# Linear attention and a routed feed-forward on one core: two blocks of transpositions moved to the head of their steps

## What is computed

```python
x = x + linear_attention(layernorm(x, g1, b1), Wq, Wk, Wv, Wo)   # 16 heads of 64, phi = elu + 1,
h = layernorm(x, g2, b2)                                          # causal sums over keys and values
x = x + gelu(h @ Wf1) @ Wf2
x = layernorm(x_in + x)
x = layernorm(x + mixture(x))     # 8 experts of width 512, the best 2 for each token
```

## Time and profile before

| | |
|---|---|
| median of 3 runs | 686.7 us (686.63 to 686.72) |
| the profiled execution's own time | 687.75 us |
| its span, first to last instruction | 686.0 us |
| TensorE busy | 651.0 us, 95% |
| VectorE busy | 530.8 us, 77% |
| ScalarE busy | 426.8 us, 62% |
| GpSimd busy | 247.1 us, 36% |
| mean granted clock of TensorE | 0.998 |

### The profile page before, as it was taken

One profiled execution on the slowest core, in us unless ns is written; L12 is line 12 of the kernel. 1 busy time (PEld: TensorE's weight loads), 2 busy tenths in 40 slices (PEclk: granted clock), 3 DMA queues, 4 the chain that ended last, 5 costly groups with the idle time before them and its releaser, 6 DMA issues.

```text
span 686.0 us, 23205 instructions
## 1 busy us (share of the span) xinstructions
PE 651.0 (95%) x9330; PEld 558.5 (81%) x9330; DVE 530.8 (77%) x1565; ACT 426.8 (62%) x862; POOL 247.1 (36%) x274
## 2 busy tenths in 40 slices
PE   3899999999999999999999999999988999999995
PEld 2678888888888788888888887877878989999983
DVE  4877788887888788888878886888788677665674
ACT  4565676558556856765585568566646666666646
POOL 6300014025313512340253134123306657766664
PEclk9999999999999999999999999999999999999999
DMA  7340010001100100100011000001031233354536
GB/s 246 106 77 18 2 33 17 18 19 49 32 10 25 49 19 18 48 18 17 19 49 33 10 27 15 18 18 33 2 96 48 72 95 118 106 156 127 171 129 185
DMA packets 46521, 40.27 MB, mean 59 GB/s; under 512 B 9104, under 2 KB 41232, under 8 KB 46416
## 3 DMA queue, kind: packets, MB, share of 16 engines
q1 hardware_dynamic: 35360, 25.25, 13.2%
q0 software_dynamic: 4784, 10.39, 4.4%
q10 hardware_dynamic: 6272, 3.16, 1.6%
HBM read 23.12 MB, written 15.66 MB: 57 GB/s over the span
## 4 chain that ended last, share of the span: by engine, by line
PE 67%; DVE 18%; ACT 8%; issue 2%; POOL 2%; DMA 1%; DVEq 0%; ACTq 0%; POOLq 0%
PE banks_o L736 9%; PE banks_sc L571 5%; PE banks_o L551 4%; PE banks_o L563 3%; PE bank_u L584 3%; PE bank_u L544 3%; DVE work L1275 3%; PE bank_q L438 3%; DVE work L1291 3%; PE bank_q L440 3%; PE bank_q L439 3%; PE bank_k L438 2%; ACT work L916 2%; PE banks_sc L438 2%; PE banks_sc L450 2%
## 5 line engine op out<-in xcount | busy, mean ns | idle before, releaser
L1743 POOL DMA_INDIRECT routed_rows<-routed,slot x64 | 63.2, 988 | 144.9 <-PE banks_sc L571 113.4
L842 ACT ACTIVATE work<-bank_u 128x384 f32<-128x384 f32 x64 | 31.5, 492 | 98.8 <-PE bank_u L584 98.5
L1291 DVE TENSOR_TENSOR work<-banks_sc,causal 128x1024 f32<-128x1024 f32 x64 | 77.7, 1214 | 0.0
L736 PE MATMUL banks_o<-w,work 128*128 x624 | 76.2, 275 | 0.0
L736 PEld LDWEIGHTS banks_o<-w,work 128*128 128x128 f32 x624 | 73.0, 192 | 0.3 <-issue 0.2
L551 PE MATMUL banks_o<-v_aug,work 128*64 128x65 f32 x2048 | 70.6, 221 | 0.0
L1711 POOL TENSOR_SCALAR ve<-mv 128x4 f32<-128x4 f32 x24 | 4.7, 196 | 170.1 <-DVE mv L1157 169.9
L551 PEld LDWEIGHTS banks_o<-v_aug,work 128*64 128x64 f32 x2048 | 65.3, 138 | 0.0
L1275 DVE SCALAR_TENSOR_TENSOR work<-bank_q,work 128x512 f32<-128x512 f32 x64 | 43.7, 683 | 22.8 <-ACT work L910 22.7
L1275 DVE SCALAR_TENSOR_TENSOR work<-bank_k,work 128x512 f32<-128x512 f32 x64 | 44.2, 690 | 21.7 <-ACT work L916 21.6
L571 PE MATMUL banks_sc<-work 64*64 64x128 f32 (+1 forms) x2048 | 56.8, 248 | 1.2 <-ACT v_aug L842 0.7
(11 more groups left out here) (331 smaller groups left out, 1807.7 us busy)
## 6 DMA issues: line engine op xcount, KB each, us to landing
work<-in_L_attn_x SPq DMA_DIRECT2D x16, 256.0 KB, 3.7
work<-routed_rows SPq DMA_DIRECT2D x20, 132.0 KB, 2.4
xg_more<-routed_rows SPq DMA_DIRECT2D x19, 132.0 KB, 2.1
stage<-in_L_ffn_w SPq DMA_DIRECT2D x8, 256.0 KB, 2.5
moe_input<-routed SPq DMA_DIRECT2D x8, 256.0 KB, 2.6
work<-moe_input ACTq DMA_DIRECT2D x8, 256.0 KB
v_aug<-expert_results SPq DMA_DIRECT2D x4, 512.0 KB, 6.4
out<-work SPq DMA_DIRECT2D x6, 256.0 KB, 2.9
```

What stands on the lines that cost most here:

```text
L736: mm = pe.matmul(Y[t % 2][:, blk(k)], hTe[t % 2][:, f, blk(k)], w2[:, bass.ds(e[t] * F + f * D, D)], start=(f == 0), stop=(f == NF - 1))
L1291: dve.tensor_tensor(am_all.rearrange("p (x m) s -> p x (m s)", m=2), sc_banks.rearrange("p (x s) -> p x s", s=2 * P), causal[:, :, :].rear ...
L1743: pool.indirect_dma_start(rows_d, bass.IndirectOffsetOnAxis(slot[:, k, c:c + 1], 0), routed[:, c, k, :], None).then_inc(sct, 16)
```

## The change

In step 2 the four transpositions of `y_t(b-1)` and their wait stand ahead of `columns(g-1)`, not behind it. In step 3 those of `front_t(b+1)` do so too, and they go to bank_q, not bank_k; their wait for the bank is `a_free` in place of `b_free`. `front_scale` reads bank_q. The wait for `h32_sb` stands ahead of `q_proj`, not `k_proj`. The call for the first sequence, ahead of all steps, keeps bank_k. Nothing is computed differently.

```diff
-            def front_t(b):
+            def front_t(b, out):
                 pe.wait_ge(ln_x[0], b + 1)
...
-                        mm = pe.transpose(bkB[:, blk(c)], xln[:, c, :], ident)
+                        mm = pe.transpose(out[:, blk(c)], xln[:, c, :], ident)
...
+                if p == 2 and not first:
+                    a_free(g - 1)
+                    y_t(b - 1, bkA)
+                if p == 3 and not last:
+                    a_free(g - 1)
+                    front_t(b + 1, bkA)
                 if g > 0:
                     columns(g - 1)
-                    if p == 2 and not first:
-                        a_free(g - 1)
-                        y_t(b - 1, bkA)
-                    if p == 3 and not last:
-                        b_free(g - 1)
-                        front_t(b + 1)
                     across(g - 1)
...
+                    if p == 3 and not last:
+                        pe.wait_ge(h32_sb, b + 2)
                     if g == 0:
                         pe.wait_ge(wlo, 5)
                     q_proj(npar, np_)
...
                 if nxt:
-                    if p == 3 and not last:
-                        pe.wait_ge(h32_sb, b + 2)
...
                     k_proj(npar, np_)
...
-                act.activation(h32, bkB[:, :], ACT.Identity, bias=cols[:, 1:2], scale=cols[:, 0:1]).then_inc(h32_sb, 1)
+                act.activation(h32, src[:, :], ACT.Identity, bias=cols[:, 1:2], scale=cols[:, 0:1]).then_inc(h32_sb, 1)
...
-                    front_scale(b + 1, True)
+                    front_scale(b + 1, True, bkA)
```

More of the change, by code:

```diff
@@ L470, in front_t @@
                     if c % 2 == 0:
-                        mm = pe.transpose(bkB[:, blk(c)], xln[:, c, :], ident)
+                        mm = pe.transpose(out[:, blk(c)], xln[:, c, :], ident)
                     else:
-                        mm = pe.matmul(bkB[:, blk(c)], xln[:, c, :], exchange, start=True, stop=True)
+                        mm = pe.matmul(out[:, blk(c)], xln[:, c, :], exchange, start=True, stop=True)
                 mm.then_inc(f1_mm, 1)
@@ L686, in _ @@
             pe.wait_ge(cst, 3)
-            front_t(0)
+            front_t(0, bkB)
             pe.wait_ge(cst, CST_ALL)
@@ L849, in y_copy, with front_scale @@
                 copy(to[:, :, 1, DH:P], at[:, :, 1, 0:DH]).then_inc(yT_sb, 1)
-            def front_scale(b, reuse):
+            def front_scale(b, reuse, src):
                 act.wait_ge(f1_mm, b + 1)
@@ L993, in _ @@
             act.wait_ge(ld_cols, 16 * 2)
-            front_scale(0, False)
+            front_scale(0, False, bkB)
             front_high(0, 0)
```

## The result

The changed kernel takes 690.96 us (median of 4, 690.56 to 692.25), the kernel before 686.71 beside it. The ratio on record is 1.0051, 95% interval 1.0034 to 1.0069: 3.5 us slower, between 2.3 and 4.7. The forecast was 691.2. The profiled execution took 690.85 us, with a span of 689.1.

The account below looks back on a forecast made before the run. The prediction took a chain through VectorE, ScalarE and GpSimd to bound steps 2 and 3, despite TensorE 95% busy. Six sequences at 0.20 + 0.52 us plus 0.20 made 4.5 us, so 691.2, range 688.6 to 693.2.

Parts of the forecast that it names:

- The chain: Steps 2 and 3 of a sequence: VectorE, ScalarE and GpSimd set the end, with TensorE on the chain only for h2_t's 0.67 us.
- the signs named: Expected in the profile: TensorE and VectorE waits in steps 2 and 3, norm2 no longer behind GpSimd, sequences 63.6 us apart.
- Step 2: y_t ahead of the columns: columns 0.90 us later, a cover of 0.70, so the states 0.20 us late per sequence.
- Step 3: front_t ahead of the columns: columns 0.94 us later, norm2's wait takes 0.42, and 0.52 us per sequence is left.
- The sum: Sequences 1 to 6 at 0.72 us each, sequence 7 at 0.20: together 4.5 us slower.
- Edits counted at nothing: The moved h32_sb wait, b_free to a_free and SyncE's load cost nothing; the first sequence 0, within 0.3 us.
- The faster one: Whole change: fewer passages between large and small matmuls on a stream TensorE bounds, 2.9 us faster, 683.8; chance 4%.
- Rival 2: The same or nearly: the states' lateness falls into waits in steps 2 and 3; 1.2 us slower, 687.9; chance 8%.
- Rival 3: Step 3: norm2's wait takes nothing because GpSimd is as late as VectorE; 7.0 us slower, 693.7; chance 8%.

Follow-up runs that it names:

- y_twice_new: The changed kernel with y_t's four transpositions issued twice, ahead of the columns: 694.66 us, ratio to before 1.0118, spacing 63.95 us.
- y_twice_old: The kernel before with y_t's four transpositions issued twice, in the old place behind the columns: 687.75 us, ratio 1.0014, spacing 62.90 us.
- y_only: The kernel before with only y_t moved ahead of the columns, measured twice: 689.51 and 689.59 us, ratios 1.0035 and 1.0032.
- bank_only: The changed kernel with both blocks back behind the columns, keeping the bank and wait edits: 686.86 us, ratio to before 0.9998.
- twice_first_new: The changed kernel with GpSimd's sum (L1721) ahead of the factor from the statistics in step 2: 690.41 us, ratio to before 1.0053.
- ffn_order: The kernel before with ffn1's second and third products exchanging banks in step 3, so the one waiting for k_phi comes third: 687.31 us, ratio 0.9997.
- order_and_twice: The kernel before with both the edit of ffn_order and that of twice_first: 684.74 us, ratio to before 0.9954.
- front_only: The changed kernel with y_t back behind the columns, so only front_t is moved, with its bank_q: 691.08 us, ratio to before 1.0044.
- twice_first: The kernel before with GpSimd's sum (L1721) ahead of the factor from the statistics in step 2: 686.82 us, ratio 0.9994.

## Why the prediction was right

**The chain.** Right. Steps 2 and 3 were bound by VectorE, ScalarE and GpSimd, and TensorE's work moved ahead of L544 went onto it (`y_twice_new` against `y_twice_old`). Of the signs named, these came: TensorE's waits ahead of `y_t` (0.24) and of the first weight load of `front_t` (0.23), VectorE's idle time ahead of the states in step 3 (0.80, forecast 0.9), `norm2` without idle time, a spacing of 63.5. The row of the states in step 2 shows no idle time, where 0.2 was forecast: `k_phis` ended at 150.16 and they started at 150.28, 0.12 later.

**Step 2.** Right in each stamp. With the shift of 0.53, `y_t` was forecast at 149.08 and came at 149.07; the columns at 149.66 and came at 149.66; the states at 150.28 and came at 150.28. Cost 0.20; `y_only` shows 0.21.

**Step 3.** Right down to `norm2`. With the shift of 0.73: `front_t` forecast 156.28, measured 156.28; columns 157.15, measured 157.10; states 157.77, measured 157.71; `norm2` 159.02, measured 158.98.

**The term that was mis-sized** is the last of that step: I took `norm2`'s lateness, 0.52, as that of `h2_t`. `h2_t` started at 160.14, where 159.05 + 0.73 + 0.52 would be 160.30. It is 0.36 late. Of the 0.16 too much, 0.04 come from the start of `norm2` and 0.11 from its length: 1.22 us in the earlier trace rows and 1.11 in the changed kernel. I had counted that length as fixed.

It is not the wait that makes `norm2` long, though the two go together in the earlier trace rows. In the kernel before, `norm2` of sequence 1 waits too and takes 1.11, and the same four instructions in `front_apply` take 1.24 without a wait:

```profile
94.93 1.11 DVE L1163 TENSOR_SCALAR work<-work,mv,rstd 128x128 f32<-128x128 f32 x4 [0.28 <-POOL work L1721]
...
145.93 1.24 DVE L1163 TENSOR_SCALAR work<-work,mv,rstd 128x128 f32<-128x128 f32 x4
146.18 0.96 POOL L1743 DMA_INDIRECT routed_rows<-routed,slot  x1 [0.30 <-issue]
...
157.91 1.07 POOL L1743 DMA_INDIRECT routed_rows<-routed,slot  x1 [0.17 <-issue]
```

What goes with the length is GpSimd: in all thirteen profiles, from 20 us on, wherever such a group of four takes 1.21 to 1.24, one of GpSimd's scatter instructions (L1743) starts 0.13 to 0.25 us behind its start, and in no group of 1.10 to 1.12 does one start in its first 0.6 us. In the changed kernel the scatter's instruction starts at 158.64, 0.34 ahead of `norm2`. That the one causes the other was not tested. Sequence 1, which has no scatter beside `norm2`, fits: there `scale2` comes 0.51 later behind `residual1` than before, and the forecast's term was 0.52.

So a sequence costs 0.20 + 0.36 = 0.56 and not 0.72. The middle distances give 63.48 - 62.90 = 0.58.

**The sum.** Worked out anew, the steps come to 6 x 0.56 + 0.20 = 3.6 us, against 4.5 forecast. In the profiles they hold 3.9: from the first `residual1` to the last `scale2` 390.08 us (88.05 to 478.13) against 386.45, so 3.63, and ahead of that 0.2 in step 2 of sequence 1 and 0.08 in sequence 0. The 0.3 above the terms lies at the edges, which I took to be like the middle: in sequence 1 `scale2` came 9.30 us after `residual1` where it was 8.79 (0.51 more; in the others 9.29 or 9.30 against 8.91 to 8.94), and the last distance grew by 0.64. The medians differ by 4.25, and the ratio gives 3.5, so the whole times can't tell 3.6 from 4.5. That the forecast of 691.2 lies 0.2 from the median is thus in part luck: a term 0.16 too large, six times over, met 0.3 that I had left out at the edges and another 0.35 between the profiles' steps and the medians, for which no row gives a cause.

**Edits counted at nothing.** Right for the wait for `h32_sb` and the bank (`bank_only`: spacing equal to 0.01). In the changed kernel `front_scale` read the bank by 158.35 and the queries' projection came at 160.56. For the first sequence I said 0 within 0.3. From step 2 to step 3 the starts of `q_proj` lie 6.84 us apart before (34.11, 40.95) and 6.92 after (33.84, 40.76): 0.08.

**Rivals.** The faster one held that TensorE bounds these steps. `y_twice_old` put 0.44 us a sequence more on TensorE there, and the spacing did not grow. So its premise is refuted, and not only its condition. Rival 2 needed `front_t` to take 0.5 us; it took 0.82 (156.28 to 157.10). Rival 3, GpSimd as late as VectorE, is refuted by `norm2`'s vanished wait and by `twice_first_new`.

## What to carry to other kernels

Ask of a block that is moved not how busy its engine is, but whose semaphore stands behind it in the stream and what that one's receiver was waiting for. Put work that nobody waits for behind the instruction that releases the next engine, and ahead of the one that waits for its answer: there 0.44 us of TensorE added nothing to the spacing. And when an instruction moves in time, do not carry its length over from the old row without a look at what the other engines did beside it: `norm2` was 0.11 us shorter once GpSimd's scatter no longer started just behind it.

## What the runs showed of the hardware

**The granted clock moved whole times by over a microsecond in places that no edit touched.** Where the attention stage hands over to the expert stage, `ffn_order` had this, by stretches (us, busy time and count of TensorE's matmuls, its weight loads, VectorE, ScalarE and GpSimd, then granted clock, DMA share, GB/s):

```profile
512.00:516.00 4.00, 2.16 (x35) 1.34 (x33) 2.97 (x13) 0.98 (x3) 0.28 (x1) 1.00 0.35 103
516.00:520.00 4.00, 4.00 (x20) 3.60 (x19) 2.23 (x6) 2.15 (x6) 3.09 (x4) 0.57 0.14 46
520.00:524.00 4.00, 4.00 (x38) 4.00 (x37) 2.37 (x11) 2.08 (x8) 1.92 (x2) 1.00 0.08 25
```

and `order_and_twice`, with the same stage:

```profile
512.00:516.00 4.00, 2.16 (x16) 1.68 (x17) 3.84 (x15) 1.36 (x3) 1.06 (x1) 1.00 0.31 76
516.00:520.00 4.00, 4.00 (x34) 3.82 (x34) 2.31 (x6) 3.60 (x10) 2.89 (x3) 1.00 0.16 51
```

After 4 us in which TensorE was busy for 2.16, the clock in one execution fell for most of the next 4 us to the lower of its two levels, 1.2 GHz (0.57 is a mean over both), and in the other it did not. In those 4 us 20 matmuls ran instead of 34. The same products of a tile follow each other by 0.21 us in the stretch at the lower clock and by 0.12 behind it:

```profile
517.34 0.41 PE L440 MATMUL banks_sc<-xT_lo,w_now_hi 128*128 128x256 f32 x1
...
517.55 0.41 PE L438 MATMUL banks_sc<-xT_hi,w_now_hi 128*128 128x256 f32 x1
...
520.12 0.28 PE L440 MATMUL bank_u<-xT_lo,w_now_hi 128*128 128x256 f32 x1
...
520.24 0.28 PE L438 MATMUL bank_u<-xT_hi,w_now_hi 128*128 128x256 f32 x1
```

From the second to the fifth copy of a tile (`xT_hi`, ScalarE L842) it took 12.52 us there, 12.25 in `front_only` and 12.58 in `y_twice_old`, whose granted clock also fell to 0.50 for two or three whole microseconds, and 10.92 to 11.05 in nine others. In `y_twice_new` it took 11.56 with the clock at 1.00; why is open. The three with the fall are 1.3 to 1.6 us longer than the nine. It is why `ffn_order`'s profiled execution has a span of 686.5 us, over the 686.0 of before, in spite of its shorter spacing.

**The mean granted clock of the timed runs goes with it.** A profile without this fall has a mean of 0.997 or 0.998 (below 1 because the clock is at the lower level in the last microseconds, when TensorE has nothing left), the three with it have 0.995 or 0.996. The last column of the table counts the runs by that. In `before` 14 of 74 lie at 0.996 or less, in `y_only` 12 of 20 over both measurements, in `ffn_order` 11 of 12, in `order_and_twice` none of 6. So the fall, or one like it, came more often in some kernels than in others, and medians of whole times under 2 us apart can't be compared without this count. Where in the program the clock of a timed run was low is not on record, and why the kernels differ in it wasn't shown.

**The start has a moment of its own.** The first projections follow each other by 0.43 us and then, from some product on, by 0.23. With the same code up to there, the first product that is followed at the short distance starts at 17.65 us in the kernel before, at 15.71 in `twice_first` and at 19.14 in `y_only`, and the first step's next projection starts 7.71 to 8.98 us after the first in the thirteen profiles. The granted clock reads 1.00 throughout this stretch in all of them, so that it is the clock that changes here is not shown.

The Trainium skill, "TensorE: Matmul & The Clock Gate", Part 1, says that activity releases the throttle and that the moment varies from run to run. The scatter at the start would agree with it in kind, though at 3 us, counted from the first product, it is wider than the page's 500 ns to either side; the rows of the granted clock do not show it.

**What stays open.** Both measurements of `y_only` lie 0.7 to 1.0 us over what its steps add to before, by the ratios and by the medians, and the changed kernel 0.35 over by its medians and 0.4 under by its ratio. For `y_only` the clock explains part at most: among the runs at 0.997 or more the medians are 689.0 (3 runs) and 689.4 (5) against 687.0 and 686.9, which is 2.0 and 2.5 us, and the steps hold 1.5. Whether moving `y_t` makes the fall of the clock more likely was not shown.
